# Moving the layer norm of output tiles, the state term and a load within the slots of a fused Mamba scan (Trainium2)

## The reference, cut to what matters

```
zxbcdt = u @ in_proj_w.T;  z, xBC, dt = split(zxbcdt)        # z 1024, x 1024, B 128, C 128, dt 64 heads
xBC = silu(causal_conv4(xBC));  dt = softplus(dt + dt_bias)
# chunks of 64 tokens: inside a chunk ("within") and from the state before it ("from before")
Y_diag = einsum(C, B, L, X*dt);  states = einsum(B, decay, X*dt);  prev = scan(states)
Y_off  = einsum(C, prev, exp(cumsum(dA)))
y  = (Y_diag + Y_off + x*D) * silu(z)
yn = y * rsqrt(mean(y*y) + 1e-5) * norm_weight
x1 = layernorm(u + yn @ out_proj_w.T)                        # rows of 512
out = layernorm(x1 + rms(ffn(x1)))
```

## Time and profile before

| what | value |
|---|---|
| median of 3 runs | 2013.19 us (2007.36 to 2015.89) |
| profiled execution, its time | 2006.9 us |
| its span | 2005.1 us |
| PE / DVE / POOL / ACT busy | 87% / 71% / 50% / 46% |
| mean granted TensorE clock | 0.919 |

### The profile page before, as it was taken

How to read it: one execution, slowest core, us unless ns; L and a number is a source line. 1 busy time by engine, 2 the same in 40 slices (tenths; PEclk the granted TensorE clock), 3 DMA queues, 4 the chain that set the end, 5 groups by cost and what they waited for, 6 DMA issues and landing times. The chain is left out here.

```text
span 2005.1 us, 37560 instructions
## 1 busy us (share of the span) xinstructions
PE 1736.9 (87%) x11168; PEld 872.1 (43%) x11168; DVE 1419.8 (71%) x2295; ACT 920.8 (46%) x1647; POOL 995.4 (50%) x1031
## 2 busy tenths in 40 slices
PE   3688889898888888888979888788999999999998
PEld 1245445444544544454544544444434334334333
DVE  6768668857857766876785776885676776766765
ACT  2453253353434335325334433434574564664753
POOL 0045436515525543543552653675674674764754
PEclk9897898898888888888889888888999999999999
DMA  6110140131123014113113202822011011010110
GB/s 203 47 47 24 40 95 26 42 68 50 37 46 88 24 40 101 31 35 79 35 42 64 66 24 52 214 49 57 17 48 63 11 52 39 29 58 26 37 43 32
DMA packets 214648, 109.35 MB, mean 55 GB/s; under 512 B 133796, under 2 KB 185696, under 8 KB 214496
## 3 DMA queue, kind: packets, MB, share of 16 engines
q1 hardware_dynamic: 214496, 107.37, 20.1%
HBM read 80.57 MB, written 26.76 MB: 54 GB/s over the span
## 5 line engine op out<-in xcount | busy, mean ns | idle before, releaser
L1024 ACT ACTIVATE decay<-ps_d 128x512 f32<-128x512 f32 x256 | 151.6, 593 | 332.5 <-PE ps_d L771 270.1
L713 PE MATMUL ps_in<-u_hi,w_hi 128*128 128x512 f16 (+1 forms) x608 | 237.3, 390 | 57.3 <-DVE u_lo L1197 35.6
L1299 DVE TENSOR_TENSOR mix<-decay,gb 128x512 f32<-128x512 f32 x256 | 224.3, 881 | 61.9 <-PE ps_yd L783 26.7
L1610 POOL TENSOR_TENSOR xend<-xpad,decay 128x256 f32<-128x256 f32 x256 | 178.7, 718 | 163.4 <-PE ps_yo L806 131.6
L735 PE MATMUL ps_in<-w_out,zg 128*128 128x512 f32 x512 | 254.3, 654 | 6.1 <-DVE pre L1210 6.1
L713 PE MATMUL ps_in<-u_lo,w_hi 128*128 128x512 f16 (+1 forms) x608 | 236.4, 389 | 0.0
L713 PE MATMUL ps_in<-u_hi,w_lo 128*128 128x512 f16 (+1 forms) x608 | 236.0, 388 | 0.0
L1210 DVE SCALAR_TENSOR_TENSOR pre<-ps_in,cws,pre 128x511 f32<-128x511 f32 (+2 forms) x240 | 178.9, 746 | 8.6 <-ACT pre L963 2.8
L793 PE MATMUL ps_yo<-bc,state 128*128 128x64 f32 x896 | 152.2, 341 | 17.2 <-DVE state L1314 17.2
L735 PEld LDWEIGHTS ps_in<-w_out,zg 128*128 128x128 f32 x512 | 108.0, 218 | 134.2 <-issue 125.4
L963 ACT ACTIVATE pre<-ps_in,cb,cws 128x512 f32<-128x512 f32 x80 | 62.2, 778 | 208.9 <-PE ps_in L713 208.8
(11 more groups left out here) (194 smaller groups left out, 3932.3 us busy)
## 6 DMA issues: line engine op xcount, KB each, us to landing
ebc<-e_dram SPq DMA_DIRECT2D x256, 64.0 KB, 2.6
u<-u_t SPq DMA_DIRECT2D x9, 1024.0 KB, 5.4
res<-u_tok SPq DMA_DIRECT2D x32, 256.0 KB, 2.7
x_dram<-res SPq DMA_DIRECT2D x32, 256.0 KB, 2.0
xa<-x_dram SPq DMA_DIRECT2D x8, 1024.0 KB, 5.5
xr<-x_dram SPq DMA_DIRECT2D x32, 256.0 KB, 2.7
out<-xr SPq DMA_DIRECT2D x32, 256.0 KB, 2.0
fw_words<-gu_words SPq DMA_DIRECT2D x32, 176.0 KB, 2.9
```

The source lines that it names most:

```text
L713: last = mm(ps_in[bk][0:m, :], w[:, k, col:col + m], u[:, k, :], start=(k == 0 and j == 0), stop=(k == KT - 1 and j == 2))
L1024: ac(decay[:, n % NG, :, :].rearrange("p a b -> p (a b)"), ps_d[n % 2][:, :], ACT.Exp).then_inc(e_done, 1)
L1299: v.tensor_tensor(mix[:, n % NG, :, :], decay[:, n % NG, :, :], gb[:, c % 2, 0:CH].unsqueeze(1).broadcast_to([P, CT, CH]), ALU.mult).then_ ...
L1610: g_.tensor_tensor(xend[:, pairs, :], xpad[:, c % 2, pairs, :], decay[:, g, :, CH - 1:CH].broadcast_to([P, CT, 2 * HD]), ALU.mult).then_in ...
```

## The change

Three things are moved, nothing is added or left out of the computation. (1) For the tiles o0 and o1, DVE's `norm_tile` goes from one slot after the output product to two slots after it, and to behind the taps of that slot; `norm_tile_end` goes from two slots after the product to four; POOL's `ln_root` and SP's `store_x1` with `load_res` follow. For o2 the same work goes behind the last chunk's `y_all`, and the end behind the taps of x7. (2) PE's `from_before` goes from the end of slot 1 of each chunk into slot 2, behind `exponents` and `aux`; on DVE the taps of slot 2 of each chunk now stand ahead of `y_before`. (3) SP issues `load_head` at slot 28 instead of 30.

```diff
+NORM_AT, NORM_END = 2, 4
@@ SP, body
-                    if n == 30 and st.proj is not None:
+                    if n == 28 and st.proj is not None:
                         load_head(b + 1)
                     for tt in range(2):
-                        if f"o{tt}" in st.at(n):
+                        if f"o{tt}" in st.at(n - NORM_END - 1):
                             store_x1(b, tt)
                             load_res(b, tt + 2)
-                    if "o2" in st.at(n):
-                        store_x1(b, 2)
+                store_x1(b, 2)
                 store_x1(b, 3)
@@ PE, body
                         new_state(b, c - 1)
+                    if g == 2 and c > 0:
+                        from_before(b, c)
                     use_in(st, n)
                     if g % 2 == 1:
                         within(b, n - 1)
                         within(b, n)
-                    if g == 1 and c > 0:
-                        from_before(b, c)
@@ DVE, use_in
-            def use_in(st, slot):
+            def use_in(st, slot, only=""):
                 for name in st.at(slot):
+                    if only and name[0] != only:
+                        continue
...
                         if int(name[1]) == TT - 1:
                             mean_square(st, TT - 1)
-                        norm_tile(st, int(name[1]))
+                            norm_tile(st, TT - 1)
@@ DVE, body
+                    if n > 0:
+                        use_in(st, n - 1)
                     if g == 2:
                         y_before(b, c)
-                    if n > 0:
-                        use_in(st, n - 1)
                     for tt in range(TT - 2):
-                        if f"o{tt}" in st.at(n - 2):
+                        if f"o{tt}" in st.at(n - NORM_AT):
+                            norm_tile(st, tt)
+                        if f"o{tt}" in st.at(n - NORM_END):
                             norm_tile_end(st, tt)
...
                 y_all(b, NC - 1)
-                norm_tile_end(st, TT - 2)
                 use_in(st, SLOTS - 1)
+                norm_tile(st, TT - 2)
...
-                use_in(st, SLOTS)
+                use_in(st, SLOTS, "x")
+                norm_tile_end(st, TT - 2)
+                use_in(st, SLOTS, "o")
@@ POOL, body
-                        if n > 0 and f"o{tt}" in st.at(n - 1):
+                        if f"o{tt}" in st.at(n - NORM_AT - 1):
                             ln_root(b, tt)
                 gate(st, NC - 1)
+                ln_root(b, TT - 2)
                 sum_squares(b, NC - 1)
```

## The result

| | before | after |
|---|---|---|
| median | 2010.28 us (4 runs, 2003.70 to 2015.89) | 2036.29 us (4 runs, 2030.42 to 2038.67) |
| ratio to before, 95% interval | | 1.0142 [1.0105, 1.0179] |
| span of the profiled execution | 2005.1 us | 2036.8 us |
| mean granted clock | 0.919 | 0.912 |

The changed kernel is 1.4% slower, where 1.4% faster was forecast. The page after, first part: PE has the same instructions and is busy 19 us longer, while DVE is busy 30 us less (the shorter `norm_tile_end`).

The account below looks back on a forecast made before the run. PE is busiest, but DVE bounds the stretch up to the next output product, and PE's gaps there halve its clock. Per batch -0.6 - 3.4 - 0.2 - 0.3 = -4.5 us, seven -31.5, last batch +1.5: -30, so 1983 us (1963 to 2023).

Parts of the forecast that it names:

- rival (b): Behind the stalls at x2 and x5: clock low about 7 us, 0.9 us more per tile; 1996 us, chance 0.17.
- the bank stall: PE waits at x2 and x5 until DVE's late norm frees the output product's bank: 3.8 us each, fourteen times.
- no gap ahead of `within`: Tile 0: PE reaches `within` at 687.6, later than DVE's chunk sum at 686.5, so no gap lowers the clock.
- the shorter norm end: In its new place o0's `norm_tile_end` takes 0.54 us instead of 1.79, saving DVE 0 to 1.25 us.
- `from_before` comes after `exponents` and `aux`, so its wait for the state is filled: PE's waits for the state, 17.2 us over 25 times, are covered; -0.6 us per batch at the place before o0.
- B: Stretch from the end of o0's output product to that of o1's: 37.2 us before, 33.8 forecast.
- C: Stretch from the end of o1's output product to that of o2's: 34.4 us before, 34.2 forecast.
- D: Stretch from the end of o2's output product to that of the next batch's o0: 92.4 us before, 91.5 forecast.
- rival (a): Stall keeps the clock low 10 us, through `within` and `from_before`; 3.4 us more lost per tile; 2031 us, chance 0.13.
- (d): Waits only exchanged: PE still waits for DVE's sum ahead of `within`, stall and gap both paid; 2008 to 2018 us, chance 0.17.

Follow-up runs that it names:

- e5: The changed kernel with ACT's exp_cs and ln_dt in slot 22 instead of 20; 1987.10 us, ratio 0.9891 to the kernel before.
- e10: The kernel before with ACT's exp_cs and ln_dt in slot 22 instead of 20; 2005.97 us, ratio 0.9997.
- e2: The changed kernel with from_before, the order of taps and y_before, and load_head back in their old places; 2052.85 us, ratio 1.0226.
- e9: The changed kernel with the adding instruction of o0's and o1's norm, from_before and the tap order in their old places; 1999.67 us, ratio 0.9957.
- e3: The changed kernel with the adding instruction of o0's and o1's norm back in the slot after the product; 1994.34 us, ratio 0.9938 to the kernel before.

## Why the prediction was wrong

How long the clock stays low behind the stall "decides this case", says the prediction; that came out at rival (b)'s 7 us and explains 0.9 us per tile. The step that failed is the one behind it: that from `within` to the end of the output product PE runs at full clock with no gap but the one it had counted. None of the three signs that were to show the prediction wrong came (the wait for L1357 missing, lows of 10 us behind it, over 2 us of wait for L1335 in slots 20 and 28); the loss came in a place that it didn't watch.

**Right: the bank stall.** Forecast 3.8 us at x2 and x5, fourteen times, 53 us; measured 3.60, fourteen times, 50.1. The low behind it was mis-sized: forecast 3.5 us, read from a single place of the kernel before, and 1.7 us of loss; measured 6.8 us behind x2's stall in all seven batches, so all of x2 ran at half speed (2.6 us). That is rival (b)'s size.

**Right: no gap ahead of `within`, and the shorter norm end.** PE came to `within` of slot 21 without a wait, and the norm's end took 0.55 us instead of 1.79 (0.54 was taken; the median of all 32 fell from 1.61 to 0.54). DVE's sum began at 687.9, 23.0 us behind o0's end, where 22.6 were forecast (686.5, with that end at 663.9). The other signs came too: POOL's wait for the variance fell from 175 to 30 us, and the waits for L1335 from 60 to 18, most of which is the 2.5 us ahead of o0 that the change leaves as they were.

**Wrong: "`from_before` comes after `exponents` and `aux`, so its wait for the state is filled".** This step counted the work of `aux` as cover and left out what `aux` itself waits for. A piece of work that is put in front of another brings its own releaser along: here ACT's copy `gb`, queued behind two table loads. The cost is 2.70 us of wait and, behind it, a low clock on `from_before` and part of o1's product, both of which the forecast had at full speed: 1.3 us (3.22 against 1.97) and some 1.9 us (9.0 against 7.13). With 0.9 us for the longer low of x2 that makes 6.8 us in B, where the forecast missed by 40.5 - 33.8 = 6.7. `e5` removes this wait and B falls to 35.1; `e10` shows that the same edit is worth nothing in the kernel before. The Trainium skill's page "ScalarE: Activation LUTs" ("Table sets: the hidden batching unit") warns of alternating functions of different sets and puts a load at about 2.7 us. In this trace each load took 1.28 us, and the instruction behind it started 0.01 us later (688.56 and 689.85), so that the two loads cost ACT 2.6 us together. The forecast didn't look at ACT's list in that slot.

**Wrong: C.** Forecast 34.2, measured 37.8. There is no table load in it. Up to the state the forecast holds: DVE's sum began 22.7 us behind o1's end (728.10; 22.8 forecast), the longer low of x5 cost nothing there, and `from_before` started with the state, as the sum in the prediction has it. The failed terms are the two behind it. `from_before` was taken at 1.8 us and the product at 7.0, their times at full clock, though PE stands waiting ahead of them; after a wait of 1.45 us they took 3.60 and 8.9 us. A low doesn't always follow that wait: in the changed kernel it lasts 6.8 us in the third to seventh batches (C 37.8), 3.4 us in the first and is absent in the second (C 34.8 in both), and in `e5` it is absent in five of seven. The five batches used for the medians repeat each other closely, so they are hardly five separate tries. What decides between the two isn't shown; in the changed kernel the low costs 3.0 us per batch.

**Right in small, with nothing left in sum: D.** Forecast -0.9, measured 0. The stretch from the first `within` of chunk 3 to o0's end gained its 0.5 us (14.62 to 14.10), and PE's wait in front of o3 fell from 0.88 to 0.63 us. The waits for row loads were 22.3 us in all instead of 16.2, but they vary from 11.3 (`e2`) to 23.5 (`e9`) among kernels that differ little there, so this can't be laid to the change.

The measured 2036 is near rival (a)'s 2031, but by luck: (a) wanted one low of 10 us behind the stall, and there were two of 6.8 us with a second gap between them, which no rival had in this place. (d) has a second gap, but ahead of `within`; that is `e2`, the norm alone. `e5`'s nearness to the forecast of 1983 is in part luck as well: its B is 1.3 us over the forecast, and its C rests on lows that didn't come. The chance given to slower, 0.14, was too small for a change that adds a wait of 3.6 us to PE fourteen times and rests on the clock forgiving it.

## What to carry to other kernels

Where PE is the bound and its clock moves, count gaps and not waits: a gap can cost itself and the half speed of what follows, so a change that moves a wait must be followed to the next wait on PE's list, down to the engine that frees each bank. Before work is moved in front of a wait as cover, look up what that work waits for on every engine, also on those that are idle half of the time. If an instruction frees a bank and three more only compute, split them: putting the freeing one back right behind the product took 42 us off the changed kernel (`e3`).

## What was not expected of the hardware

Matmuls without any use made the kernel faster: 16 repeats (3.4 us at full clock) inside the stalls took 41 us off 2036, and filling gaps in the kernel before took 1.4% off it. Table loads took 1.28 us each. The Trainium skill's page "TensorE: Matmul & The Clock Gate" ("Seeing it yourself" and "HAM oscillation") describes the drop for idle gaps of several us; in this case a wait of 1.45 us behind busy PE was followed by a low (1.00 before, 0.50 for the 6.7 us shown above) in six batches of the changed kernel and by none in one, and by none in five of seven in `e5`.
